# A graph network on one core: narrower windows for the edge counts of layer 0, and their ring cleared by ScalarE

## The reference

```
# layer 0: messages from the source row and the relation of the edge's type
m = clifford_linear(h[src] * relation_emb[edge_type], msg_w, msg_b) * gate * norm
h_agg = segment_sum(m, dst)
x1 = layernorm(x + clifford_linear(x + h_agg, upd_w, upd_b))
# layers 1 to 3: the mean over a node's in-edges, three times over the same graph
conv(h) = segment_sum(h[src], dst) / max(deg, 1) @ Wl.T + bl + h @ Wr.T
x2 = layernorm(x1 + conv2(relu(conv2(relu(conv1(x1))))))
```

## Time and profile before

| What | Value |
|---|---|
| median of three timed executions | 3848.27 us |
| lowest, highest | 3825.55, 3861.35 us |
| span of the profiled execution | 3293.7 us |
| difference of the median and the span | 554.6 us |
| layer 0, by the timeline (first gather to last node) | about 173 to 1577 us |
| mean granted TensorE clock | 0.935 of full speed |

### The profile page before, as it was taken

The page is one execution under the profiler, slowest core; times in us unless marked ns, Lnnn a source line. Parts: engine busy times, 40 slices in busy tenths (PEclk is TensorE's granted clock), DMA queues, the critical chain, the costliest instruction groups (busy, mean ns, idle before and its releaser), DMA issues. The chain is left out here.

```text
span 3293.7 us, 54777 instructions
## 1 busy us (share of the span) xinstructions
PE 2864.3 (87%) x16731; PEld 2464.3 (75%) x16731; DVE 2458.8 (75%) x5529; ACT 2224.0 (68%) x3945; POOL 2351.4 (71%) x2185
## 2 busy tenths in 40 slices
PE   6559999999999989997599999669999957999985
PEld 4448877787778878786488888558888846888884
DVE  7968888888888888887466667546666745787786
ACT  1057777777777777774577877468877836777771
POOL 6267777777777777773577777567777756777773
PEclk6579999999999999998799999889999978999997
DMA  4256666665556666663766666376666647666662
GB/s 136 73 133 168 173 165 167 167 167 165 167 164 168 165 173 167 168 169 113 228 196 201 199 194 188 105 246 207 201 195 197 184 134 225 204 210 205 206 185 89
DMA packets 335600, 573.59 MB, mean 174 GB/s; under 512 B 47029, under 2 KB 231686, under 8 KB 335302
## 3 DMA queue, kind: packets, MB, share of 16 engines
q0 software_dynamic: 101088, 277.97, 30.4%
q1 hardware_dynamic: 230697, 289.55, 28.1%
q10 hardware_dynamic: 3517, 2.48, 0.3%
HBM read 491.85 MB, written 77.97 MB: 173 GB/s over the span
## 5 line engine op out<-in xcount | busy, mean ns | idle before, releaser
L1483 POOL DMA_INDIRECT rows_arena<-table_h,src_idx x1128 | 1236.6, 1096 | 483.8 <-issue 364.0
L2052 PE MATMUL bank<-wide_counts,h_pairs 128*128 128x512 f32 (+1 forms) x4116 | 945.7, 384 | 123.6 <-ACT wide_counts L1632 104.0
L1483 POOL DMA_INDIRECT rows_arena<-table_scaled_x,src_idx x782 | 839.0, 1073 | 285.8 <-issue 273.6
L2052 PEld LDWEIGHTS bank<-wide_counts,h_pairs 128*128 128x128 f32 x4116 | 735.4, 193 | 262.9 <-issue 128.3
L1989 PE MATMUL bank<-rel_pairs,ftype_hot 125*128 125x258 f32 x4688 | 711.0, 299 | 51.3 <-ACT ftype_hot L1610 51.0
L1989 PEld LDWEIGHTS bank<-rel_pairs,ftype_hot 125*128 125x128 f32 x4688 | 620.6, 191 | 85.5 <-ACT ftype_hot L1610 51.1
L1632 ACT CAST wide_counts<-rows_arena 128x1024 fp32r<-128x1024 bf16 (+1 forms) x525 | 549.8, 1047 | 68.0 <-DMA rows_arena<-edge_counts 67.9
L1832 DVE TENSOR_TENSOR h_pairs<-rows_arena,h_pairs 128x512 fp32r<-128x512 f32 (+1 forms) x525 | 352.9, 682 | 259.6 <-ACT h_pairs L1629 254.9
L1824 DVE TENSOR_TENSOR row_pairs<-rows_arena,row_pairs 128x1024 fp32r<-128x1024 f32 x282 | 343.1, 1218 | 208.8 <-ACT row_pairs L1619 202.5
L1629 ACT CAST h_pairs<-rows_arena 128x512 fp32r<-128x512 f32 (+1 forms) x525 | 320.9, 611 | 197.3 <-PE bank L2052 152.9
L1653 ACT CAST rows_arena<-bank 128x448 bf16<-128x448 f32 (+1 forms) x812 | 368.3, 505 | 119.3 <-PE bank L2038 74.9
(11 more groups left out here) (186 smaller groups left out, 3098.9 us busy)
## 6 DMA issues: line engine op xcount, KB each, us to landing
rows_arena<-edge_counts SPq DMA_DIRECT2D x234, 512.0 KB, 4.0
edge_counts<-fcount SPq DMA_DIRECT2D x52, 832.0 KB, 6.3
rows_arena<-in_edge_type_dram SPq DMA_DIRECT2D x195, 187.5 KB
rows_arena<-table_h SPq DMA_DIRECT2D x36, 512.0 KB, 11.9
rows_arena<-table_h,src_idx POOLq DMA_INDIRECT x1128, 3.6
rows_arena<-table_scaled_x,src_idx POOLq DMA_INDIRECT x782
table_h<-chunk_info SPq DMA_DIRECT2D x96, 128.0 KB, 4.0
rows_arena<-edge_counts SPq DMA_DIRECT2D x39, 256.0 KB, 3.1
```

The source lines that it names most:

```text
L1483: pool.indirect_dma_start(out=rows[:, g % ring, c, :], out_offset=None, in_=table[:, :], in_offset=bass.IndirectOffsetOnAxis(ap=src_idx[:, ...
L2052: last = pe.matmul(bank[2 + h][:, 0:cols_of(w)], h_pairs[:, v % HALVES, part, b % HALF, h * P:(h + 1) * P], wide_counts[:, v % HALVES, b % ...
```

## The change

A chunk's counts span `CHUNK_W = 13` destinations instead of 16. With it, `KEY_W` becomes 52 and `KEYS` 676; the products have 7 x 52 = 364 and 6 x 52 = 312 columns; the ring's rows have (256 + 13) x 4 = 1076 values instead of 1088. The pieces and the number of stores and clears stay.

The clearing of a piece goes from VectorE to ScalarE. ScalarE does it behind the copies of the same chunk `i`: it waits for the old store, and writes the 13 x 256 16-bit values as 13 x 128 32-bit words (`count_words`, a view of the ring), as a copy of a tile of ones scaled by 0.0. VectorE still waits for `s_zeroed` before the addition.

```diff
@@ -59,7 +59,7 @@
 ROW_PAIRS = 2
 HALF, HALVES = 2, 3
 RING0, RING = 4, 4
-CHUNK_W = 16
+CHUNK_W = 13
 HTILE = 4
 ATILES = 2
 EARLY = 10
@@ -1393,6 +1393,7 @@
                     key_hot = lent_seg("key_hot").bitcast(BF16).rearrange("p (r w) -> p r w", r=COUNT_HOTS)
                     count_ring = sb("fcount", [P, TPW, (COUNT_RING + CHUNK_W) * HTILE], BF16, tmp)
                     overhang = count_ring[:, :, COUNT_RING * HTILE:(COUNT_RING + CHUNK_W) * HTILE]
+                    count_words = count_ring[:, :, :].bitcast(F32)
                     for k in range(LAPS, STORES):
                         assert chunks_for_store(k - LAPS) <= first_touch[k]
                         if k % LAPS == 0:
@@ -1644,6 +1645,17 @@
                                 act.copy(window_sum[:, w % 2, 0:sum_cols],
                                          seg_bank[w % 2][:, 0:sum_cols]).then_inc(s_evac, 1)
 
+                        def clear_counts(i):
+
+                            for k in range(LAPS, STORES):
+                                if first_touch[k] == i:
+                                    act.wait_ge(s_count_out[k % LAPS], 16 * (k // LAPS))
+                                    words = STORE_COLS * HTILE // 2
+                                    at = k % LAPS * words
+                                    act.activation(count_words[:, :, at:at + words],
+                                                   ones[:, 0:words].unsqueeze(1).to_broadcast([P, TPW, words]),
+                                                   ACT.Copy, scale=0.0).then_inc(s_zeroed, 1)
+
                         def stage_count(i):
 
                             act.wait_ge(s_count, i + 1)
@@ -1653,6 +1665,7 @@
                                 last = act.copy(staged[:, i % STAGES, lo:hi, :].rearrange("p t w -> p (t w)"),
                                                 bank[2 + h][:, 0:(hi - lo) * KEY_W])
                             last.then_inc(s_staged, 1)
+                            clear_counts(i)
 
                         def sqrt_var(b):
                             act.wait_ge(s_var, b + 1)
@@ -1795,12 +1808,6 @@
 
                         def count_add(i):
 
-                            for k in range(LAPS, STORES):
-                                if first_touch[k] == i:
-                                    dve.wait_ge(s_count_out[k % LAPS], 16 * (k // LAPS))
-                                    at = k % LAPS * STORE_COLS * HTILE
-                                    old = count_ring[:, :, at:at + STORE_COLS * HTILE]
-                                    dve.tensor_scalar(old, old, float(P * GC), None, ALU.is_gt).then_inc(s_zeroed, 1)
                             cleared = sum(first_touch[k] <= i for k in range(LAPS, STORES))
                             if cleared:
                                 dve.wait_ge(s_zeroed, cleared)
```

## The result

The changed kernel takes 3871.01 us in the median of 14 executions (3848.19 to 3906.22), the kernel before, run beside it, 3838.98 us (3823.84 to 3871.26, also 14). The ratio is 1.0079, with a 95% interval of [1.0054, 1.0104]: 0.8% slower, which is little but more than the interval leaves to chance, where 1.2% faster was forecast. Ratios are of the fast executions of both kernels alone, and so can differ a little from the quotient of the medians given.

What follows compares the result with a forecast made beforehand. GpSimd's back-to-back gathers in layer 0 were taken as the bound. Off 3848.3 us came 29 (clears), 15 (shorter addition and comparison) and 3 (last group's lag), 47 in all: 3801 us, own range 3785 to 3815, whole range 3755 to 3838.

Steps and rivals of the forecast that it cites:

- Step 1: Layer 0: without VectorE's 48 clears, GpSimd's gathers are no longer stretched by them, 29 us off (bounds 0 and 29.0).
- Step 2: Layer 0: ScalarE takes 48 clears of 1.58 us, 76 us in all, net +34 us there, nothing on the path.
- slower rival: ScalarE's clears delay the type hots, TensorE stalls and the row ring holds GpSimd: about 3900 us, chance 0.09.
- Steps 3 and 4: Count addition falls to 501 ns, key comparison by 44 ns on VectorE; GpSimd's gathers are held less, 15 us off together.
- Step 5: TensorE's count products get 46 and 40 ns shorter, 35 us off its work, 0 off the path.
- more comes off: Gathers fall into step with VectorE's bursts and miss the sensitive places: 38 us more off, 3763 us, chance 0.17.
- it is given back: TensorE or its ScalarE chain takes over the pace, or ScalarE's clears hold gathers: 20 us gained, 3828 us, chance 0.24.

Runs made afterwards that it cites:

- e5: The kernel before, unchanged, profiled on chip 1: 3856.75 us (one time), span 3854.1 us.
- e1: The kernel before, unchanged, profiled again on chip 5: 3299.89 us, ratio 0.9998 to the kernel before.
- e4: Clears moved to ScalarE, windows kept at 16, against the kernel before on chip 5: 3262.80 us, ratio 0.9886.
- e9: The changed kernel with ScalarE's 48 clears left out, on chip 2: 3860.75 us, ratio 1.0027 to the kernel before.
- e6: Clears moved to ScalarE, windows kept at 16, against the kernel before on chip 1: 3839.49 us, ratio 0.9973.
- e3: Windows narrowed to 13, clears left on VectorE, against the kernel before on chip 5: 3272.43 us, ratio 0.9916.
- e2: The changed kernel, unchanged, run again on chip 5: 3236.68 us, ratio 0.9814 to the kernel before.
- e10: The kernel before with half of its relation products (low part of the table left out), on chip 2: 3811.54 us, ratio 0.9909 to the kernel before.
- e8: Windows narrowed to 13, clears left on VectorE, against the kernel before on chip 2: 3856.42 us, ratio 1.0047.

## Why the prediction failed, point by point

**The step that failed** is "The profiled span is 3293.7 us; the median of the timed runs, 3848.27, has 554.6 us more around it, which I leave as they are". It took a profile and times of two different levels as one execution with 554.6 us around it, and with that it took the bound of the profiled level, "at GpSimd's pace", for the bound of the timed runs. The gap was in plain sight: 17% of the span. In every execution of this study whose time and span both are known, at either level, they differ by 1.9 to 5.6 us. With the gap unexplained, the sum should have been made conditional on the timed executions having the stage of the profile. They don't: the stage takes 1317 us at the lower level and 1608 at the upper, and layers 1 to 3 take 642, 649 and 690 us in e5, against 569, 563 and 593 in e1.

**Step 1, the clears leave VectorE** (29 us). By e4 the chain loses 22.9 us. In the changed kernel at the lower level no gather lasts as long as the longest of the earlier trace rows. The timeline there shows a clear of ScalarE with a gather inside it at its floor:

```profile
259.62 1.62 ACT L1655 ACTIVATE fcount<-ones 128x1664 f32<-128x1664 f32 x1
260.13 0.94 POOL L1484 DMA_INDIRECT rows_arena<-table_scaled_x,src_idx  x1 [0.30 <-issue]
```

91 gathers overlap a clear in that profile and are 10.1 us over the floor together, 0.11 us each, where the 51 of before were 0.57 each (29.0 us). 49 of the 91 are at the floor, and of the others all but one end where a VectorE instruction lets them go (below). ScalarE writing the same tile leaves gathers alone. Right: the clears' 29 us are gone in e4 too, but other VectorE instructions there take 6 us more than before, since the gathers now meet them at other moments. So the term was 6 us too large.

**Step 2, the clears on ScalarE** (1.58 us each, nothing on the path). 1.609 us each, 48 of them, 77.2 us. The copies fell to 457 and 425 ns, by 70 and 59 where 56 and 48 were forecast. Nothing waits for them at the lower level, and at the upper e9 shows no cost. The least distance from a copy's end to its addition, read as 7.3 us, is 6.5 at the first clear, which is cover enough as well. The slower rival, a clear ahead of the type hots, has e4 and e6 against it, where the clears alone cost nothing at either level, and e9.

**Steps 3 and 4, the narrower addition and comparison** (501 ns, 15 us off the gathers). 507 ns, and 17.2 us of chain by e3. Here the forecast set the row against the Trainium skill: "SBUF — State Buffer", section "Who interferes with whom", infers that a tensor_tensor doesn't lock GpSimd's descriptor writing out, and the forecast took from this that an addition holds no gather up, which would have left 5 us. It called the rows undecided, since a comparison follows each addition. Now they decide. The comparison shrank from 432 to 395 ns and the addition from 586 to 507, so the gathers stretched beside such a burst tell which end they follow. With windows of 16 (the given profile, e1, e4) they end 0.82 us behind the addition and 0.31 us behind the comparison; with windows of 13 (e2, e3) 0.82 us behind the addition and 0.35 us behind the comparison. The distance to the addition is 0.815 to 0.824 us in all five profiles (10th to 90th percentile), the one to the comparison moves by what the comparison lost. And 20 of those in the given profile have neither the key comparison nor the small one of line 1792 behind their addition, and end at 0.81 to 0.83 us all the same. One of the gathers in the changed kernel at the lower level, where the gather ends at 241.44, the addition at 240.62 and the comparison at 241.09:

```profile
240.11 0.51 DVE L1819 TENSOR_TENSOR fcount<-fcount,rows_arena 128x676 bf16 x1
240.26 1.18 POOL L1484 DMA_INDIRECT rows_arena<-table_scaled_x,src_idx  x1 [0.30 <-issue]
...
240.70 0.39 DVE L1806 TENSOR_SCALAR rows_arena<-iota_key,chunk_info 128x676 bf16<-128x676 f16 x1
```

There are 154 such gathers in the given profile (with those near clears, which the forecast's 117 left out), 47.5 us over the floor, and 143 in e2, 31.6 us: a ratio of 0.67, where the square of the durations said 0.73. As only the beginning of a gather is held, the 0.13 us go off both durations: (0.507 - 0.13)^2 / (0.586 - 0.13)^2 is 0.68, by an estimate from these rows.

The addition does hold gathers up, but not every one beside it: what counts is which started first. Of the gathers of the given profile that start while an addition runs (from 0.05 us behind its start to 0.15 us before its end), 131 of 132 end 0.79 to 0.85 us behind its end and none lasts its ordinary 0.95 us; of those that start 0.05 to 0.4 us before the addition, and so run through much of it, 63 of 68 last under 0.96 us. Such a one, in the kernel before:

```profile
460.73 0.94 POOL L1483 DMA_INDIRECT rows_arena<-table_scaled_x,src_idx  x1 [0.30 <-issue]
460.93 0.59 DVE L1812 TENSOR_TENSOR fcount<-fcount,rows_arena 128x832 bf16 x1 [0.24 <-issue]
```

The addition thus holds only a gather's beginning, the first 0.13 us (0.945 less 0.82), not what follows. Two f32 instructions show what it takes. The window comparison of line 1735, which reads two tiles of SBUF, leaves none of the 78 gathers that start while it runs at the floor, and the message that reads both inputs from SBUF none of 30 (68 and 26 end at the same distance behind it). The message whose relation rows come from TensorE's bank, in PSUM, leaves 55 of 58 at the floor. The same section of the Trainium skill says that a VectorE instruction with two SBUF inputs contends with a GpSimd instruction that reads SBUF; a gather reads its row indices (`src_idx`) there, and the trace agrees. Its inference on descriptor writing isn't refuted: the forecast had read it as if it covered the whole gather. The key comparison, with one input, holds gathers as well: 90 of the 107 that start while it runs end 0.79 to 0.85 us behind its end.

**Step 5, the products** (46 and 40 ns less). 34 and 29 ns less, 329 and 299 ns; off the path at the lower level, as said.

**The sum.** 47 us were forecast at GpSimd's pace; the lower level gave 62 by the medians, 51.2 of them in the chain, 4.9 in the tail (the last group's first message now starts at 1477.09, 4.9 us behind the last gather's end, where it was 9.8) and the rest later. Of the difference to 47, 11 us come from the two parts together being more than apart: 17.2 + 22.9 = 40.1 against 51.2 in the chain (by the medians 26 and 36 do add up to the 62, so each part alone gained more outside it). By what holds each gather, from the given profile to e2: clears 29.0 us less, additions 48.6 to 32.0, key comparisons 8.9 to 2.2, and the window comparisons of line 1735, which no step mentions, 13.6 to 20.6, so 7 us more. In e3 the additions hold 16.2 us less and the window comparisons 9.9 us more. The rival "more comes off" named such a step; it had 38 more, it got a quarter of that. That the 15 us of steps 3 and 4 came out near is thus partly luck. The gathers' mean is 1.016 us where 1.02 was named, VectorE is busy for 1049 us where 1035 was. At the lower level the steps held; the executions that were timed ran under another bound.

**At the upper level** the nearest rival is "it is given back", in that another chain than GpSimd's has the pace. Neither its price nor its mechanism fits as it stands: it had the limit of TensorE's work 18 to 35 us short of GpSimd's pace, but the stage was some 290 us longer than at that pace before the change was made, and e10 shows that TensorE's work isn't the limit. From e5 to the changed kernel the gathers shrink by 55 us, and the gaps between them grow from 262 us over the ordinary ones to 328. That the result is 0.6 to 0.8% above the kernel before, and not equal to it, goes with the width (e8). What goes along with it is the wait of ScalarE's copies put to "remote" (300 to 1500 us): 92.7, 127.7 and 151.0 us in the profiles with windows of 16 (e5, e6, e10), and 160 to 207 us in the six with windows of 13. That it is the cause isn't shown, and why narrower windows should lengthen it isn't known.

**What stays open** is the upper level itself. Each chip was used in one set, and all medians of a set had its level; whether the level belongs to the chip or to the occasion isn't separated. Shown is that VectorE, ScalarE and GpSimd are busy in layer 0 for as long as at the lower level within 3%, and the DMA engines with the packets of the gathers' queue over the whole span too (26.3% of 3854.1 us in e5, 30.7% of 3297.4 us in e1), that engines which wait for TensorE's products start microseconds behind the products' recorded ends, and that neither half the relation matmuls, nor the absence of the clears, nor the depth of the ring takes this away. When a DMA has landed is mostly not recorded there. Whether TensorE really ends later than its records say (their ends are modelled), or its signals arrive late, the profile can't tell: it lacks the record of the release itself.

## What to carry to other kernels

Set the span of the profile against the time of the runs before anything else. Here the difference was 1.9 to 5.6 us wherever both were of one execution; one of 17% meant that profile and times were of different levels, and then no bound read from the profile may be carried to the times without a condition and a chance of its own. And judge a bound by what it leaves unused: a chain that leads by the depth of its ring is the pace only while its consumer keeps up. Gaps in which it waits for a free buffer show that the consumer doesn't; a run with the ring a step deeper and one a step shallower then tell whether the depth itself costs time. And when a fast instruction lasts longer at times, sort the cases by which of the two engines started first, and by where the other's inputs lie.

## What was not expected of the hardware

- One program takes 3299 us in the runs on one chip and 3844 to 3852 us in those on three others. VectorE, ScalarE and GpSimd are busy as long within 3% in layer 0; they wait for TensorE's results, with 450 to 521 us of late messages in layer 0 where the lower level has none.
- A VectorE addition of two bf16 operands in SBUF stretches an indirect DMA instruction of GpSimd that starts while it runs (131 of 132 end 0.79 to 0.85 us behind the addition's end), and not one that was running before (63 of 68 at the floor). A VectorE product with one input in PSUM leaves 55 of 58 at the floor, and a ScalarE write of 1664 words to the same tile holds none.
- Where TensorE's products come late, the depth of the gathers' ring makes no difference: with five, four and three groups of rows the changed kernel takes 3860.8, 3862.6 and 3857.5 us (four on another chip of the same level), and the waits for a free group stay at 258 to 276 us.
- A stall of TensorE costs twice: its granted clock goes from 1.00 to 0.52 behind one, and over layer 0 it is 0.90 to 0.92 (0.86 in e10) against 0.99 at the lower level.
